# Turning the rows of queries and keys with DMAs, in a macaron block on one core

## The reference

```
x = x + 0.5 * ffn(layernorm(x))
x = x + attention(layernorm(x))
x = x + 0.5 * ffn(layernorm(x))

ffn(x):        hidden = silu(x @ wu.T) * (x @ wg.T); return hidden @ wd.T
               # wu, wg: 1024 x 256, wd: 256 x 1024, each weight made ternary (-1, 0, 1 times a scale)
attention(x):  q, k, v = x @ wq, x @ wk, x @ wv      # 16 heads of 16 numbers
               q, k = rope(q), rope(k)
               out = softmax(causal(q @ k.T / 4)) @ v
               return out @ wo
```

## Time and profile before

| | |
|---|---|
| median of 3 runs | 941.23 us (940.11 to 943.03) |
| the profiled execution, its own time | 944.56 us |
| its span in the trace | 942.8 us |
| busy PE, DVE, ACT, POOL | 787.1, 744.7, 635.5, 552.4 us |
| PE weight loads | 600.4 us |
| mean granted clock of TensorE | 0.937 |
| mean DMA traffic | 16 GB/s |

### The profile page before, as it was taken

One profiled execution on the slowest core, in us unless ns is written; L12 is line 12 of the kernel. 1 busy time (PEld: TensorE's weight loads), 2 busy tenths in 40 slices (PEclk: granted clock), 3 DMA queues, 4 the chain that ended last, 5 costly groups with the idle time before them and its releaser, 6 DMA issues.

```text
span 942.8 us, 19902 instructions
## 1 busy us (share of the span) xinstructions
PE 787.1 (83%) x7488; PEld 600.4 (64%) x7488; DVE 744.7 (79%) x1640; ACT 635.5 (67%) x1349; POOL 552.4 (59%) x535
## 2 busy tenths in 40 slices
PE   0437889898998989898989999898989899878866
PEld 0225556777677677676777767776767677556544
DVE  3744486989889898989898898989898988767652
ACT  2104467877777777877787777777787777767542
POOL 1036574766667676666676666767676666644221
PEclk9959777999999999999999999999999999979787
DMA  8300000000000000000000000000000000000000
GB/s 308 101 1 1 1 1 2 1 13 1 4 10 2 12 2 13 1 12 2 13 2 13 1 1 13 2 12 2 13 2 13 1 13 1 13 1 13 1 12 12
DMA packets 9949, 15.10 MB, mean 16 GB/s; under 512 B 640, under 2 KB 9088, under 8 KB 9344
## 3 DMA queue, kind: packets, MB, share of 16 engines
q1 hardware_dynamic: 9280, 11.54, 3.6%
q10 hardware_dynamic: 576, 2.29, 0.6%
HBM read 9.63 MB, written 4.19 MB: 15 GB/s over the span
## 4 chain that ended last, share of the span: by engine, by line
PE 45%; DVE 31%; ACT 12%; issue 7%; POOL 4%; DMA 1%; DVEq 0%; POOLq 0%; SPq 0%; ACTq 0%
PE misc_ps L370 9%; PE down_ps L370 6%; PE up_ps L370 6%; PE gate_ps L370 5%; PE probt_ps L435 4%; PE score_ps L389 4%; DVE neg_max L856 4%; PE pv_ps L417 3%; PE score_ps L385 3%; DVE hid L922 3%; PE misc_ps L482 3%; DVE exp_bias L862 3%; DVE silu_b L911 3%; ACT prob L624 2%; DVE attn L894 2%
## 5 line engine op out<-in xcount | busy, mean ns | idle before, releaser
L1015 POOL TENSOR_TENSOR hid_l<-hid,hid_h 128x512 f16<-128x512 f32 x128 | 148.5, 1160 | 264.8 <-ACT hid_h L639 250.0
L615 ACT ACTIVATE prob_h<-probt_ps 128x384 f16<-128x384 f32 x256 | 127.2, 497 | 102.2 <-PE probt_ps L435 101.0
L624 ACT ACTIVATE prob<-score_ps,exp_bias,exp_scale 128x256 f32<-128x256 f32 x256 | 146.6, 573 | 1.6 <-DVE exp_bias L862 1.4
L1008 POOL TENSOR_TENSOR prob_l<-prob_t,prob_h 128x384 f16<-128x384 f32 x128 | 117.9, 921 | 48.5 <-ACT prob_t L619 47.9
L435 PE MATMUL probt_ps<-ident_f,prob 128*128 128x128 f32 x768 | 134.2, 286 | 13.0 <-ACT prob_t L619 13.0
L370 PE MATMUL up_ps<-xt_hi,tern_up 128*128 128x256 f16 x512 | 128.1, 287 | 19.8 <-DVE tern_up L694 12.7
L370 PE MATMUL down_ps<-tern_down,hid_h 128*128 128x256 f16 x512 | 122.4, 278 | 19.1 <-POOL hid_l L1015 18.3
L370 PE MATMUL up_ps<-xt_lo,tern_up 128*128 128x256 f16 x512 | 128.1, 287 | 0.0
L370 PE MATMUL gate_ps<-xt_hi,tern_gate 128*128 128x256 f16 x512 | 124.9, 282 | 1.8 <-DVE tern_gate L694 1.8
L370 PE MATMUL gate_ps<-xt_lo,tern_gate 128*128 128x256 f16 x512 | 124.1, 281 | 0.0
L911 DVE SCALAR_TENSOR_TENSOR silu_b<-tanh_b,up_ps 128x512 f32<-128x512 f32 x128 | 87.1, 681 | 46.4 <-ACT tanh_b L633 46.4
(11 more groups left out here) (108 smaller groups left out, 1992.3 us busy)
## 6 DMA issues: line engine op xcount, KB each, us to landing
xs<-x SPq DMA_DIRECT2D x16, 256.0 KB, 3.0
out<-xs SPq DMA_DIRECT2D x16, 256.0 KB, 2.1
raw_gate<-w_gate_t ACTq DMA_DIRECT2D x1, 1024.0 KB, 8.4
raw_up<-w_up_t SPq DMA_DIRECT2D x1, 1024.0 KB, 7.8
raw_down<-w_down_t SPq DMA_DIRECT2D x1, 1024.0 KB, 10.4
raw_w<-wqkvo ACTq DMA_DIRECT2D x1, 1024.0 KB, 12.9
cos<-rope_cos SPq DMA_DIRECT2D x1, 512.0 KB, 14.0
sin<-rope_sin SPq DMA_DIRECT2D x1, 512.0 KB, 14.7
```

The source lines that it names most:

```text
L615: act.activation(prob_h[:, pair % 2, j, :], probt_ps[:, 0:384], ACT.Copy).then_inc(prob_h_done, 1)
L624: act.activation(prob[:, s % 2, j, 0:256], score_ps[:, j, 0:256], ACT.Exp, bias=exp_bias[:, j:j + 1], scale=exp_scale[:, :])
L1008: pool.tensor_tensor(prob_l[:, pair % 2, 0, :], prob_t[:, pair % 2, :], prob_h[:, pair % 2, 0, :], ALU.subtract).then_inc(prob_l_done[0], 1)
L1015: pool.tensor_tensor(hid_l[:, s % 2, :, :].rearrange("p m n -> p (m n)"), hid[:, s % 2, :], hid_h[:, s % 2, :, :].rearrange("p m n -> p (m ...
```

## The change

The transposes and their copies go, and the SP queue turns the rows by four DMAs a batch, `turn_rows`, each waiting for the low parts. The keys are laid out in `k_row` as 16 heads x 128 numbers, of which a head fills one half (by the head's parity) and the other half stays zero, from a memset of POOL at the start. Turned, they are planes of 128 partitions (`k_pad`), one for each head, and the score matmuls read 128 partitions of both. Keys are written by two instructions of 8 heads on ACT and on POOL where one of 16 stood. ACT waits for the DMAs of the batch before ahead of writing rows, SP for the scores of two batches before, and PE for the four DMAs ahead of the first scores of a step.

```diff
-    ("out_proj", 2, "a", 3), ("v", 2, "b", 1), ("norm3", 3, "b", 3), ("stack_q0", 5, "a", 1),
-    ("stack_k0", 5, "b", 1), ("stack_q1", 6, "a", 1), ("stack_k1", 6, "b", 1), ("norm1", 7, "a", -1),
+    ("out_proj", 2, "a", 3), ("v", 2, "b", 1), ("norm3", 3, "b", 3), ("norm1", 7, "a", -1),
...
-        k_row = sb("k_row", [P, NT, HEADS, 4, HD], F16)
+        k_row = sb("k_row", [P, NT, HEADS, 2 * STK], F16)
         q_stk = sb("q_stk", [P, 2, SLOTS, SEQ], F16)
-        k_stk = sb("k_stk", [P, 2, SLOTS, SEQ], F16)
+        k_pad = sb("k_pad", [P, 2, HEADS, SEQ], F16)
...
+        def row_parts(tile, m, places):
+            if m == 0:
+                return [q_row[:, tile, :, places, :]]
+            pairs = k_row[:, tile, :, :].rearrange("p (s j) c -> p s j c", j=2)
+            return [pairs[:, :, j, STK * j:STK * (j + 1)].rearrange("p s (a d) -> p s a d", d=HD)[:, :, places, :]
+                    for j in range(2)]
...
-            engine.wait_ge(row_hi_done, st.at(lambda t: 4 * (t - 1) + 2 * tile + m + 1))
-            engine.tensor_tensor(row[:, tile, :, places, :], r[:, :, None, :].to_broadcast([P, HEADS, 2, HD]),
-                                 row[:, tile, :, 0:1, :].to_broadcast([P, HEADS, 2, HD]), ALU.subtract
-                                 ).then_inc(row_lo_done[m][tile], 1)
+            engine.wait_ge(row_hi_done, st.at(lambda t: 6 * (t - 1) + 3 * tile + (3 if m else 1)))
+            dsts = row_parts(tile, m, (slice(1, 3), slice(1, 4, 2))[m])
+            highs = row_parts(tile, m, slice(0, 1))
+            step = len(dsts)
+            for j in range(step):
+                heads = HEADS // step
+                engine.tensor_tensor(dsts[j], r[:, j::step, None, :].to_broadcast([P, heads, 2, HD]),
+                                     highs[j].to_broadcast([P, heads, 2, HD]), ALU.subtract
+                                     ).then_inc(row_lo_done[m][tile], 1)
...
-            for b in range(NBATCH):
-                sp.wait_ge(ffn2_added, b + 1)
-                sp.dma_start(out_dram[b], rows(b)).then_inc(out_stored, 16)
+            def turn_rows(b, tile):
+                cols = slice(tile * P, (tile + 1) * P)
+                sp.wait_ge(row_lo_done[0][tile], b + 1)
+                if b >= 2 and tile == 0:
+                    sp.wait_ge(scores_done, SLOTS * (b - 1))
+                sp.dma_start_transpose(q_stk[:, b % 2, :, cols],
+                                       q_row[:, tile, :, :, :].rearrange("p h a d -> p (h a d)")).then_inc(stk_loaded[tile], 16)
+                sp.wait_ge(row_lo_done[1][tile], 2 * (b + 1))
+                sp.dma_start_transpose(k_pad[:, b % 2, :, cols],
+                                       k_row[:, tile, :, :].rearrange("p h c -> p (h c)")).then_inc(stk_loaded[tile], 16)
+
+            for t in range(1, LAST_STEP + 1):
+                if live(t - 4):
+                    sp.wait_ge(ffn2_added, t - 3)
+                    sp.dma_start(out_dram[t - 4], rows(t - 4)).then_inc(out_stored, 16)
+                if live(t - 1):
+                    for tile in range(NT):
+                        turn_rows(t - 1, tile)
...
-                pe.wait_ge(misc_taken, st.at(lambda t: misc_through(t - 1, "stack_k1")))
+                if s == 0:
+                    for tile in range(NT):
+                        pe.wait_ge(stk_loaded[tile], 32 * (st.first - 1))
...
-                    q = q_stk[STK * j:STK * (j + 1), par, s, :]
-                    k = k_stk[STK * j:STK * (j + 1), par, s, :]
+                    q = q_stk[:, par, s, :]
+                    k = k_pad[:, par, 2 * s + j, :]
...
                 act.wait_ge(rope_done, st.at(lambda t: 2 * (t - 1) + tile + 1))
+                if st.live(2):
+                    b = st.first - 2
+                    act.wait_ge(stk_loaded[tile], 32 * (b + 1))
+                elif tile == 0:
+                    act.wait_ge(pad_zeroed, 1)
...
-                for m, (row, places) in enumerate(((q_row, slice(0, 4, 3)), (k_row, slice(0, 4, 2)))):
-                    dst = row[:, tile, :, places, :]
-                    src = r[:, m, :, None, :].to_broadcast([P, HEADS, 2, HD])
-                    act.activation(dst, src, ACT.Copy).then_inc(row_hi_done, 1)
+                for m, places in enumerate((slice(0, 4, 3), slice(0, 4, 2))):
+                    dsts = row_parts(tile, m, places)
+                    step = len(dsts)
+                    for j in range(step):
+                        act.activation(dsts[j], r[:, m, j::step, None, :].to_broadcast([P, HEADS // step, 2, HD]),
+                                       ACT.Copy).then_inc(row_hi_done, 1)
...
-                dve.tensor_copy(ident_h[:, :], ident_f[:, :]).then_inc(casts_done, 1)
...
+            pool.memset(k_row[:, :, :, :].rearrange("p n h c -> p (n h c)").bitcast(F32), 0.0).then_inc(pad_zeroed, 1)
             pool.wait_ge(casts_done, 1)
```

More of the change, by code:

```diff
@@ L61 @@
     ("norm2", 0, "a", 1), ("qk0", 0, "b", 1), ("qk1", 1, "a", 1), ("attn_t", 1, "b", 3),
[2 rows of a table removed]
+    ("out_proj", 2, "a", 3), ("v", 2, "b", 1), ("norm3", 3, "b", 3), ("norm1", 7, "a", -1),
 ]
-STACK_DVE = ("stack_k0", "stack_q0", "stack_q1")
 PE_SLOT = ["scores", "product_v", "misc_a", "transpose_0", "up", "gate", "transpose_1", "misc_b",
@@ L180, in macaron_kernel @@
         ident_f = sb("ident_f", [P, P])
-        ident_h = sb("ident_h", [P, P], F16)
         ident_b = sb("ident_b", [P, P], BF16)
@@ L269, in macaron_kernel @@
         misc_ps = ps("misc_ps", [P, 512])
-        misc_h16 = misc_ps[:, :].bitcast(F16)
         x_loaded = [sem("x_even_loaded"), sem("x_odd_loaded")]
@@ L279, in macaron_kernel @@
         wmax_done, wmax_all, split_done = sem("wmax_done"), sem("wmax_all"), sem("split_done")
-        casts_done, ones_done = sem("casts_done"), sem("ones_done")
+        casts_done, ones_done, pad_zeroed = sem("casts_done"), sem("ones_done"), sem("pad_zeroed")
+        stk_loaded = [sem("stk_even_loaded"), sem("stk_odd_loaded")]
         scales_done, w_scales_done = sem("scales_done"), sem("w_scales_done")
@@ L328, in row_lo @@
                 return
-            row, places = ((q_row, slice(1, 3)), (k_row, slice(1, 4, 2)))[m]
             r = rope_r[:, tile, :].rearrange("p (m h d) -> p m h d", m=2, d=HD)[:, m]
-            engine.wait_ge(row_hi_done, st.at(lambda t: 4 * (t - 1) + 2 * tile + m + 1))
-            engine.tensor_tensor(row[:, tile, :, places, :], r[:, :, None, :].to_broadcast([P, HEADS, 2, HD]),
-                                 row[:, tile, :, 0:1, :].to_broadcast([P, HEADS, 2, HD]), ALU.subtract
-                                 ).then_inc(row_lo_done[m][tile], 1)
+            engine.wait_ge(row_hi_done, st.at(lambda t: 6 * (t - 1) + 3 * tile + (3 if m else 1)))
[7 more added lines that the diff above has]
+                                     ).then_inc(row_lo_done[m][tile], 1)
         x_dram = x.rearrange("b (n p) e -> b p n e", p=P)
@@ L521, in misc @@
                             mm = split_product(misc_ps[:, tile * E:(tile + 1) * E], pairs, tile == 0)
[L522 to L530, removed]
                     mm.then_inc(misc_written, 1)
@@ L551, in _ @@
             pe.wait_ge(ident_loaded, 16)
-            run_steps(pe, step, before={1: lambda: pe.wait_ge(casts_done, 4)})
+            run_steps(pe, step, before={1: lambda: pe.wait_ge(casts_done, 3)})
         @block.scalar
@@ L595, in misc @@
                                        scale=QKV_OUT).then_inc(v_hi_done, 1)
-                    elif name.startswith("stack") and name not in STACK_DVE:
-                        copy_stack(act, st, name, lag, lambda dst, src: act.activation(dst, src, ACT.Copy))
             def rope_hi(st, tile):
@@ L839, in misc @@
                         low_part(st, lag, attn_l, attn_h, attn_h_done)
-                    elif name in STACK_DVE:
-                        copy_stack(dve, st, name, lag, dve.tensor_copy)
                     elif name == "v":
```

## The result

| | before | after |
|---|---|---|
| median | 940.72 us (940.11 to 943.03, 4 runs) | 888.13 us (883.8 to 891.44, 4 runs) |
| the profiled execution, its own time | 944.56 us | 886.57 us |
| its span | 942.8 us | 884.8 us |
| mean granted clock | 0.937 | 0.951 |

The ratio of the means is 0.9434, with an interval of 0.9387 to 0.9481. The kernel is faster by 52.6 us; the forecast was 43 less than the 941.2 of before, 898, with a range of 870 to 940. Of the seven runs of the kernel before that stand beside the first four experiments one was in a slow state and took 2509.2 us; the ratios leave it out, and without it their median of 942.66 us is 942.45.

A forecast was written before the change was run, and what follows sets the result against it. PE (46.2 us) and DVE (45.4) were near full in a 50.8 us step, neither alone the limit. 944.6 - 31 - 15 = 898.6, less 3.3 to the median, 895, rounded up to 898 us; range 870 to 940.

The forecast's parts named there:

- The sum: Whole kernel: 944.6 - 31 - 15 = 898.6, less 3.3 against the median, 895, rounded up to 898 us; steady step about 48.
- Part 1: Stack transposes and copies go: 1.9 us a batch on the chain, 16 batches, 31 us; bounds 16 and 40.
- Part 2: Score matmuls use all 128 rows: a half 0.28 us for 0.48, 29 us possible, half taken, 15; ends 0 and 35.
- the third rival: Chain time moves to the other engine or DMA traffic slows reads: 925 us, to 941 with lower clock; chance 0.12.
- The ends: Steps at both ends, with few batches under way, hide more of the gain, so 895 was rounded up to 898 us.
- Slots: Sign of being right: slots 5 and 6 of a step shorter by 0.7 and 1.2 us.
- Part 3: Work added on ACT and POOL by split key instructions and zeroing: 0 us; 10 if cover in slots 4 and 5 were gone.
- Part 4: Transposing DMAs on SP's queue and their waits: 23 ns a piece, 8.8 us a step, in time, 0 us on the path.
- The late-DMA rival: Ahead of slot 0's scores PE waits for DMAs: at 58.5 ns a piece 9.1 us late a step, 1044 us; chance 0.12.
- One block at a time: SP's queue pays a landing per 128x128 block: 101 us a step, 1800 us, or 1190 by the page's price; chance 0.08.
- The gain is eaten: Same as the third rival: half of Part 1 (16 us) and nothing of Part 2, 925 us, to 941; chance 0.12.

The follow-up runs named there:

- the first four experiments: Kernels run in a group beside the kernel before, whose median over seven runs there was 942.66 us; the text does not list the four.
- part 1 alone: Against the kernel before: rows turned by DMA, but keys stay narrow and score matmuls read 64 partitions; 928.13 us, ratio 0.9839.
- part 2 alone: Kernel before with score matmuls over all 128 partitions of its own stacks, heads not separated, so output differs; 917.22 us, ratio 0.9732.
- three planes: Kernel after with key blocks 192 numbers apart, written by one instruction of 16 heads, DMA turning 24 blocks a tile, not 16; 894.66 us, ratio 0.9493.
- probabilities first: Kernel after with POOL, in slot 5, making a low part of probabilities ahead of the low parts of the rows; 903.7 us, ratio 0.957.
- the kernel with four turnings: Kernel after with each key DMA issued four times, the copies going to dead weight buffers; 1062.86 us, ratio 1.1276.
- Nine matmuls: Nine unread mask matmuls in PE's idle time of slot 3: added to the kernel after, 886.47 us; added to part 1 alone, 918.07 us.

## Why the prediction was right, and where not

**The sum.** Undisturbed steps, so that the clock stays out:

| | forecast | measured |
|---|---|---|
| part 1 alone | 1.9 | 50.8 - 48.9 = 1.9 |
| part 2 alone | 0.9 (of 1.8) | 50.8 - 49.6 = 1.2 |
| part 2 on top of part 1 | | 48.9 - 47.4 = 1.5 |
| both | 2.8 (step of 48) | 50.8 - 47.4 = 3.4 |

**Part 1, 31 us.** Right in the step, to a tenth. Alone it gave 14.5 us, since PE, rid of the transposes, idled more and the clock fell more often. With part 2 beside it most of that loss is absent. So the medians aren't additive: 14.5 and 25.4 alone, 52.6 to 56.1 together. A slip of the sum changes nothing: three copies of 0.6 and the transposes of 0.62 are 2.4 us and not "the full 2.0"; the term is what stands on the chain, 0.60 + 0.61 + 0.62 + 0.09 = 1.9. The prediction had named the lower level of the clock in the third rival, at 1.2 us for a step that has it; that size was right (47.4 to 48.6), but that part 1 alone would have it in nearly every step wasn't foreseen.

**Part 2, 15 us.** This is the term that was mis-sized. The mechanism held in every point: 0.11 from mask to score, 0.27 to 0.28 a half where halves stand back to back. In the timeline of PE of the kernel after:

```profile
353.49 0.27 PE L403 MATMUL score_ps<-mask_b,ident_b 128*128 128x256 bf16 x1
353.60 0.27 PE L407 MATMUL score_ps<-k_pad,q_stk 128*128 128x256 f16 x1
...
353.77 0.27 PE L403 MATMUL score_ps<-mask_b,ident_b 128*128 128x256 bf16 x1
...
370.50 0.28 PE L403 MATMUL score_ps<-mask_b,ident_b 128*128 128x256 bf16 x1 [0.42 <-ACT prob L641]
```

I had halved 1.8 us a step because DVE had only 0.7 left in slot 7 and would wait for PE and ACT. What came is 1.2 to 1.5, two thirds to five sixths. The last row shows what probably takes the rest: the second half of a pair waits for ACT to empty the scores. This wait of PE grew from 9.9 us in all to 24.9, but that it is what the rest was lost to wasn't shown. The cut for "another engine will be late" was right in kind and too deep. In the step that is 0.6 us more than forecast, 16 x 0.6 = 9.6 us, about the whole of the error against 898 (9.9 us); the range held the result.

**The ends.** Rounding up to 898, "since the steps at both ends hide more", was wrong: the stretches before the first and behind the eleventh store, six of the 16 batches' worth, gave 9.6 + 14.0 = 23.6 us, 3.9 a batch, and the ten steps between 3.4 each.

**Slots.** Forecast: slots 5 and 6 shorter by 0.7 and 1.2 us. Measured 1.4 and 1.4, with slot 7 longer by 0.5, so slots 5 to 7 together are shorter by 2.3 and the rest of the 3.4 is in slots 0 to 4, where the score matmuls had the chain. The chain of the step after shows what is late in the middle of it, in time order:

```profile
367.05 1.16 POOL hid_l L1027
368.21 1.12 POOL q_row L334
369.33 1.26 POOL k_row L334 x2
370.60 0.88 POOL prob_l L1020
...
371.97 0.46 PE pv_ps L435 x12
```

In slot 5 POOL carries the chain now and hands it to PE. Neither edit to POOL's load and order (three planes, probabilities first) made the step shorter, so no experiment here gains by easing POOL; neither is free of side effects, so it isn't excluded as a bound either.

**Part 3, 0 us.** Not contradicted. The groups of the kernel after:

```profile
L334 POOL TENSOR_TENSOR k_row<-rope_r,k_row 128x256 f16<-128x256 f32 x64 | 41.6, 672 | 0.0
L622 ACT ACTIVATE k_row<-rope_r 128x256 f16<-128x256 f32 x64 | 23.3, 422 | 0.0
...
L1063 POOL MEMSET k_row<- 128x2048 f32 x1 | 1.8, 1804 | 0.3 <-POOLq L1102 0.3
```

The split costs 2 x 672 - 1160 = 184 ns a tile on POOL (0.20 forecast) and 2 x 422 - 637 = 207 on ACT, at the upper end of the 0.1 to 0.2 forecast; the line through ACT's two rows would have given 0.08. The memset took 1.8 us and the reduction behind it still has 9.6 us of idle time ahead of it.

**Part 4, 0 us on the path.** Right, with 22.8 ns a piece for the 23 read from two queues' packets, and 7 us of room. So close a hit is in part luck: the 0.6% of q10 is a rounded number, and with anything from 0.55 to 0.65% the same line gives 18 to 28 ns, all of which are in time. The late-DMA rival didn't happen, and the kernel with four turnings shows that it was a real one: 174 us more. Its price of 58.5 ns a piece was wrong by 2.6 times.

**One block at a time.** Refuted by the landings: 3.2 us for 8 blocks of 128x128 and 4.4 us for 16, (4.4 - 3.2) / 8 = 0.15 us for a further block. The 1309 ns of the Trainium skill, page "VectorE: DVE Perf Modes", section "The three transpose paths", isn't borne out for a block among several. By the same line a first block costs 3.2 - 7 x 0.15 = 2.2 us with its fixed part, and a single block by itself was not run. By the prediction's estimate from that figure, paid block after block, it would have been 1190 us; the measurement decides.

**The gain is eaten.** No: the chain did move from PE and DVE to ACT (12% to 30%) and POOL (to 12%), but after 3.4 us a step, not before.

## What to carry to other kernels

Price a transposing DMA between on-chip buffers by its 256-byte pieces (23 ns each on one of 16 engines here), compare that with the time between the last producer and the first reader, also in the short steps at the ends, and leave it on a queue with nothing behind it. Matmuls on 64 rows between matmuls on 128 cost 0.10 us at each change here; zeros in the unused half removed it, with PE's busy time smaller and not larger. Compare undisturbed steps when judging an edit, and look for idle time of PE ahead of any stretch with a lower granted clock: a few unread matmuls there gave 10 us in one kernel of this study, and nothing clear of noise in another.

## What the runs showed that was not expected

- Part 1 alone lowered the clock: its mean granted clock is 0.924, that of the kernel before 0.937. It isn't PE's amount of work that decides: part 2 alone and both parts together, in which PE is busy for less still (43.6 and 41.9 us of an undisturbed step, against 44.2 with part 1 alone and 46.2 before), are at 0.956 and 0.951. A low stretch costs 1.0 us (48.9 to 49.9) to 1.2 us (47.4 to 48.6) of a step. Nine matmuls, about 1 us of PE, removed the one behind them. Why the kernel with both parts has fewer low stretches than that with part 1 alone wasn't tested.
- The change of rows costs on both sides: 0.10 us going to 64 rows (0.21 for 0.11) and 0.09 going back (0.15 for 0.06).
- The turning DMAs hold SP's queue for 1.2 us (8 blocks, in a steady step) and 1.6 to 3.2 us (16, median 2.0), far longer than the 0.37 to 0.39 us of a plain store there; nothing but the next DMA is behind them.
- The price of a piece didn't change with load: 22.8 ns where a step has a DMA share of 0.20 and 23.0 where it has 0.49.
